# A graph kernel's count matrix: stored by lane in quarters, and block degrees from wide products with a masked sum

## What is computed

```python
def gcn_conv(x, src, dst, W, b):
    n = x.shape[0]
    h = x @ W
    ones = jnp.ones(src.shape[0], dtype=x.dtype)
    deg = jax.ops.segment_sum(ones, dst, num_segments=n)
    dinv = jnp.where(deg > 0, jax.lax.rsqrt(deg), 0.0)
    norm = dinv[src] * dinv[dst]
    msgs = h[src] * norm[:, None]
    out = jax.ops.segment_sum(msgs, dst, num_segments=n)
    return out + b
...
h = gcn_conv(x, src, dst, W1, b1)
h = gcn_conv(h, src, dst, W2, b2)
return jax.nn.relu(h)
```

## Time and profile before

| | us |
|---|---|
| median of 3 runs | 6543.93 |
| lowest, highest | 6538.44, 6555.55 |
| the profiled execution | 6502.53 |
| its span on the page | 6500.8 |

### The profile page before, as it was taken

The page is one execution under the profiler, slowest core; times in us unless marked ns, Lnnn a source line. Parts: engine busy times, 40 slices in busy tenths (PEclk is TensorE's granted clock), DMA queues, the critical chain, the costliest instruction groups (busy, mean ns, idle before and its releaser), DMA issues. The chain is left out here.

```text
span 6500.8 us, 161934 instructions
## 1 busy us (share of the span) xinstructions
PE 4790.6 (74%) x32887; PEld 3107.1 (48%) x32888; DVE 4860.5 (75%) x21938; ACT 3979.7 (61%) x10577; POOL 4009.3 (62%) x5381
## 2 busy tenths in 40 slices
PE   1466666666666666664999999999938888886699
PEld 0233344334343433432555555555525556554699
DVE  6577777777677777773999999999976677777333
ACT  3355555555455545543999999999967777776100
POOL 1277777777677777764666666666627777776000
PEclk8588888878788778876999999999969999998799
DMA  8755556556455555555333333333317777775698
GB/s 224 239 186 182 186 193 197 184 191 194 160 188 174 175 170 167 176 162 160 72 72 72 72 73 74 73 73 73 73 37 216 217 217 223 213 219 174 258 360 344
DMA packets 1161941, 1090.82 MB, mean 168 GB/s; under 512 B 750004, under 2 KB 1023523, under 8 KB 1142980
## 3 DMA queue, kind: packets, MB, share of 16 engines
q1 hardware_dynamic: 1033656, 684.89, 38.9%
q0 software_dynamic: 88560, 320.26, 13.2%
q10 hardware_dynamic: 39580, 84.01, 3.4%
HBM read 658.14 MB, written 430.64 MB: 167 GB/s over the span
## 5 line engine op out<-in xcount | busy, mean ns | idle before, releaser
L914 POOL DMA_INDIRECT rows<-rowS,idx x1616 | 1949.0, 1206 | 787.9 <-issue 441.0
L1185 PE MATMUL psa<-one_c,one_s 128*128 128x392 bf16 x2352 | 605.1, 372 | 762.8 <-DVE one_s L996 461.4
L2425 PE MATMUL psm<-msg,onem 128*128 128x260 f32 x3648 | 918.0, 395 | 205.9 <-issue 169.7
L1694 DVE CUSTOM_DVE_ANT_0 junk<-bufh,attb 128x64 bf16<-128x64 f32 x5472 | 1043.5, 238 | 14.1 <-ACT bufh L1742 6.4
L2346 POOL TENSOR_TENSOR msg<-oj,heads 128x512 f32<-128x512 f32 x760 | 799.3, 1074 | 208.7 <-DMA oj<-rows 176.3
L988 DVE TENSOR_TENSOR one_c<-ioc,pairS 128x1176 bf16<-128x1176 f16 x784 | 598.4, 763 | 433.4 <-remote 227.7
L2425 PEld LDWEIGHTS psm<-msg,onem 128*128 128x128 f32 x3648 | 649.6, 190 | 474.0 <-issue 397.7
L1078 ACT ACTIVATE lgS<-preS 128x1024 f32<-128x1024 f32 x404 | 413.4, 1023 | 617.4 <-PE preS L1174 268.3
L1071 ACT ACTIVATE cnts<-psa 128x392 bf16<-128x392 f32 x784 | 366.8, 490 | 661.2 <-remote 344.3
L1782 PE MATMUL pre<-P3h,oneT 128*128 x5472 | 757.0, 275 | 0.0
L1659 POOL TENSOR_SCALAR one<-io128b,side 128x128 bf16<-128x128 bf16 x912 | 695.7, 763 | 67.2 <-DMA side<-rows 41.0
(11 more groups left out here) (306 smaller groups left out, 9392.0 us busy)
## 6 DMA issues: line engine op xcount, KB each, us to landing
oj<-rows SPq DMA_DIRECT2D x912, 256.0 KB
adj<-adj SPq DMA_DIRECT2D x70, 1568.0 KB, 9.7
adj<-cnts ACTq DMA_DIRECT2D x49, 1568.0 KB
side<-rows SPq DMA_DIRECT2D x912, 69.0 KB, 2.3
bufh<-rows SPq DMA_DIRECT2D x912, 64.0 KB, 2.3
eaS<-in_edge_attr_dram SPq DMA_DIRECT2D x201, 256.0 KB
low<-dlow SPq DMA_DIRECT2D x202, 252.0 KB
adj_early<-adj SPq DMA_DIRECT2D x28, 1568.0 KB, 8.7
```

The lines of the kernel that those rows point to most:

```text
L914: eng.indirect_dma_start(out=m["rows"][h], out_offset=bass.IndirectOffsetOnAxis(ap=idx[s][:, k:k + 1], axis=0), in_=rows[s][:, k, :], in_o ...
L1185: mm = eng.matmul(psa[r][:, 0:z.GC], one_s[r][:, k, :], one_c[r][:, k, :], start=(k == 0), stop=(k == GT - 1))
L1694: ins = eng.tensor_tensor_reduce(junk[q][:, k * H + h, 0, :], buf[j][:, k, 1, h * D:(h + 1) * D], attb[:, 1, h, :], 1.0, 0.0, ALU.mult, AL ...
L2425: mm = eng.matmul(psm[j][:, 0:C + H], one[q][:, k, :], msg[q][:, k, :], start=(k == 0), stop=(k == UT - 1))
```

## The change

`cnts` is laid out by lane, [128 lanes, 49 source blocks]. A copy of ACT now fills 8 whole lanes, 392 numbers in a row in each partition, and reads its PSUM tile with the two dimensions swapped. So a quarter of the lanes (LANES = 32) is complete after each step, and ACT issues a store of that quarter (392 KB) at the end of every step, after waiting for its own copies. The tile in DRAM and the tiles that conv_stage loads have the same layout; a product there takes its weights as `adj[j][:, :, s]`, one number in every 49.

The degrees no longer use each part as weights. Twelve matmuls of four source blocks (512 columns) and one of a single block (128), with the square of ones as weights and `cnts` as moving operand, sum into the PSUM tile `turned`, in which every partition then has the column sums. They stand at the end of step 0, after its last count matmul. In step 1, after `rank`, DVE multiplies `turned` with the identity repeated DEG = 4 times and sums the 512 products of each partition. PE's next use of `turned` that could run into this, the turn for step 2, waits for DVE's product.

```diff
@@ spread_stage, vector
-                if closes(b, s):
-                    eng.wait_ge(deg_ready, b)
-                    eng.tensor_copy(m["deg"][:, span(b - 1, 1)], psr[:, (K + 1) * HB:(K + 1) * HB + 1])
...
+            def degrees(b):
+
+                eng.wait_ge(deg_ready, b)
+                eng.wait_ge(deg_kept, b)
+                eng.tensor_tensor(degm[:, :, :], turned[:, :, :],
+                                  m["ident"][:, None, :].to_broadcast([P, DEG, P]), ALU.mult).then_inc(deg_read, 1)
+                eng.wait_ge(deg_read, b)
+                eng.tensor_reduce(m["deg"][:, span(b - 1, 1)], degm[:, :, :].rearrange("p c l -> p (c l)"), AX.X,
+                                  ALU.add).then_inc(deg_kept, 1)
...
                 rank(b, s, h, between)
+                if closes(b, s):
+                    degrees(b)
@@ spread_stage, scalar
-                        wait(eng, stored[u], b // 2 * 16)
+                        wait(eng, stored[u], b // 2 * 16 * NR_BUF)
...
-                eng.activation(cnts[u][:, :, GQ * s + q, :], psa[r][:, 0:z.GC].rearrange("p (t d) -> p t d", d=GD),
+                eng.activation(cnts[u][:, span((GQ * s + q) * GD, GD), :],
+                               psa[r][:, 0:z.GC].rearrange("p (t d) -> p d t", d=GD),
                                ACT.Copy).then_inc(copied[q], 1)
...
-                    if s == NR_BUF - 1:
-                        for q in range(GQ):
-                            eng.wait_ge(copied[q], step(b, s) + 1)
-                        to = m["adj"][b] if isinstance(b, int) else m["adj"][bass.ds(b, 1)].rearrange("o p c -> (o p) c")
-                        eng.dma_start(to, cnts[u][:, :, :, :].rearrange("p s g d -> p (s g d)")).then_inc(stored[u], 16)
+                    for q in range(GQ):
+                        eng.wait_ge(copied[q], step(b, s) + 1)
+                    to = m["adj"][b] if isinstance(b, int) else m["adj"][bass.ds(b, 1)].rearrange("o p c -> (o p) c")
+                    eng.dma_start(to[:, s * LANES * NB:(s + 1) * LANES * NB],
+                                  cnts[u][:, s * LANES:(s + 1) * LANES, :].rearrange("p l c -> p (l c)"))\
+                       .then_inc(stored[u], 16)
@@ spread_stage, tensor
+                if s == 2 and (not isinstance(b, int) or 0 < b <= NB):
+                    eng.wait_ge(deg_read, b)
...
-                if closes(b, s):
-                    for q in range(GQ):
-                        eng.wait_ge(copied[q], t - 1)
-                    for c in range(NB):
-                        mm = eng.matmul(psr[:, (K + 1) * HB:(K + 1) * HB + 1],
-                                        cnts[1 - u][:, c, :, :].rearrange("p g d -> p (g d)"), m["onesb"][:, 0:1],
-                                        start=(c == 0), stop=(c == NB - 1), skip_group_check=True)
-                    mm.then_inc(deg_ready, 1)
...
+            def degrees(b, u):
+
+                for q in range(GQ):
+                    eng.wait_ge(copied[q], NR_BUF * b)
+                eng.wait_ge(evacuated, NR_BUF * b + 2)
+                for c in range(0, NB, DEG):
+                    n = min(DEG, NB - c)
+                    mm = eng.matmul(turned[:, 0:n, :], m["onesb"][:, :],
+                                    cnts[u][:, :, c:c + n].rearrange("p l c -> p c l"),
+                                    start=(c == 0), stop=(c + n == NB), skip_group_check=True)
+                mm.then_inc(deg_ready, 1)
...
                 if u is not None:
                     adj(b, s, 3)
+                if s == 0 and (not isinstance(b, int) or 0 < b <= NB):
+                    degrees(b, 1 - (after_u if u is None else u))
@@ conv_stage, tensor
             def product(n, j, s):
-                return eng.matmul(place(j), adj[j][:, s, :], parts[n][:, s, :, :].rearrange("p r d -> p (r d)"),
+                return eng.matmul(place(j), adj[j][:, :, s], parts[n][:, s, :, :].rearrange("p r d -> p (r d)"),
                                   start=(s == 0), stop=(s == NB - 1))
```

More of the change, by code:

```diff
@@ L45 @@
 GQ = GB // NR_BUF
+LANES = GQ * GD
 CODE = 1024
@@ L48 @@
 WIDE = 4
+DEG = 4
 EXACT = 256
@@ L258, in gnn_kernel @@
             message_stage(nc, z, m, sb, ps, sem)
-            m["early"] = [sb(top, f"adj_early{j}", [P, NB, P], bf16, side="right") for j in range(EARLY)]
+            m["early"] = [sb(top, f"adj_early{j}", [P, P, NB], bf16, side="right") for j in range(EARLY)]
             node_stage(nc, z, m, sb, ps, sem, W1)
@@ L757, in spread_stage @@
         one_c = [sb(ctx, f"one_c{r}", [P, GT, z.GC], bf16) for r in range(2)]
-        cnts = [sb(ctx, f"cnts{u}", [P, NB, GB, GD], bf16) for u in range(2)]
+        cnts = [sb(ctx, f"cnts{u}", [P, P, NB], bf16) for u in range(2)]
         turned = ps(ctx, "turnedS", [P, K // 2, P], fp32)
@@ L774, in spread_stage @@
             "pre_ready", "exp_done", "out_ready"))
-        deg_ready = sem(ctx, "deg_ready")
+        degm = sb(ctx, "degm", [P, DEG, P], fp32)
+        deg_ready, deg_read, deg_kept = (sem(ctx, n) for n in ("deg_ready", "deg_read", "deg_kept"))
         stored = [sem(ctx, f"adj_stored{u}") for u in range(2)]
@@ L1051, in _ @@
                 eng.memset(oh[j][:, K, :], 0.0).then_inc(cleared, 1)
+            eng.memset(degm[:, :, :], 0.0).then_inc(deg_kept, 1)
             hots(0, 0)
@@ L1127, in _ @@
             for u in range(2):
-                eng.wait_ge(stored[u], (NB + 1 - u) // 2 * 16)
+                eng.wait_ge(stored[u], (NB + 1 - u) // 2 * 16 * NR_BUF)
         @block.tensor
@@ L1138, in turn, with count @@
                 mm.then_inc(turned_ready, 1)
-            def count(b, s, u):
+            def count(b, s):
                 j = s % 2
@@ L1201, in body @@
                 if exists(*nxt):
-                    count(*nxt, (after_u if u is None else u if s < NR_BUF - 1 else 1 - u))
+                    count(*nxt)
                 if u is not None:
                     adj(b, s, 3)
+                if s == 0 and (not isinstance(b, int) or 0 < b <= NB):
+                    degrees(b, 1 - (after_u if u is None else u))
             def one(b, u):
@@ L1215, in _ @@
             turn(0, 0)
-            count(0, 0, 0)
+            count(0, 0)
             rounds(eng, NB // 2, two)
@@ L2512, in _ @@
             for j in range(EARLY):
-                eng.dma_start(m["early"][j][:, :, :].rearrange("p s d -> p (s d)"), m["adj"][j]).then_inc(adj_in, 16)
+                eng.dma_start(m["early"][j][:, :, :].rearrange("p d s -> p (d s)"), m["adj"][j]).then_inc(adj_in, 16)
             eng.wait_ge(adj_in, 16 * EARLY)
@@ L2664, in conv_stage @@
         parts = [m["parts0"], sb(ctx, "parts1", [P, NB, PARTS, D], bf16)]
-        adj = m["early"] + [sb(ctx, f"adj{j}", [P, NB, P], bf16) for j in range(EARLY, BC)]
+        adj = m["early"] + [sb(ctx, f"adj{j}", [P, P, NB], bf16) for j in range(EARLY, BC)]
         bias = [sb(ctx, f"cb{n}", [P, D], fp32) for n in range(2)]
@@ L2704, in load @@
                     a = m["adj"][b] if isinstance(b, int) else m["adj"][bass.ds(b, 1)].rearrange("o p c -> (o p) c")
-                    eng.dma_start(adj[j][:, :, :].rearrange("p s d -> p (s d)"), a).then_inc(adj_in[j], 16)
+                    eng.dma_start(adj[j][:, :, :].rearrange("p d s -> p (d s)"), a).then_inc(adj_in[j], 16)
             for j in range(EARLY, BC):
-                eng.dma_start(adj[j][:, :, :].rearrange("p s d -> p (s d)"), m["adj"][j]).then_inc(adj_in[j], 16)
+                eng.dma_start(adj[j][:, :, :].rearrange("p d s -> p (d s)"), m["adj"][j]).then_inc(adj_in[j], 16)
             eng.wait_ge(w_zero, 1)
```

2 lines of the change are left out of this document (1 added, 1 removed).

## The result

The changed kernel takes **6784.64 us** (median; 6781.08 to 6797.31) where the kernel before takes 6541.18 beside it: a ratio of 1.0378, 95% interval 1.0347 to 1.0409. It is slower by 243 us. The prediction said 6372, 6290 to 6640. Where the runs of one kernel fall into two groups more than 1.5% apart, a ratio compares the faster group alone.

What follows compares the result with a forecast made beforehand. DVE with its stalls (39.8 + 13.9 us a block) was the bound, POOL (48.7) next. Blocks going from 53.75 to 50.2 us over 49 blocks, convolutions 0, gave 6544 - 172 = 6372 us; range 6290 to 6640.

Steps and rivals of the forecast that it cites:

- Part (3): Degrees on PE: 13 wide matmuls replace 49 one-column ones, taking 2.7 to 5.5 us a block, 10.3 at the slow end.
- Rival D: Degree matmuls crawl and the stall before the ranks stays: 57.5 us a block, +184 us, 6728 us; chance 0.08.
- Part (5): DVE's 7.41 us stall before L967 comes from PE's one-column burst, perhaps with the store, and goes.
- the gain of 172 us: Whole forecast saving, all in the first stage: blocks fall from 53.75 to 50.2 us, over 49 blocks.
- Without the stalls POOL sets the block: First stage: once DVE's stalls go, POOL's 32 scatters set a block of 49.7 us, 50.2 with waits left over.
- Part (1): Store of 1568 KB split into four of 392 KB: pair-load waits go, ACT's extra at least 1 us a block.
- Part (2): Copy into cnts (L1071) with strided PSUM read: taken as 0.49 us, bounds 0.4 to 0.98.
- Part (4): DVE's degree product and sum over 512 numbers: at most 726 and 716 ns, +1.3 us a block.
- Part (6): Convolutions: strided weight loads stay hidden under the 82.5 ns product, costing 0; bound 130 ns, +228 us.
- rivals B and C: Convolutions paced by strided loads: 107 ns a product, 6490 us (chance 0.13); or above 118 ns, bound 6600 us (0.10).

Runs made afterwards that it cites:

- e9: Changed kernel with its 13 degree matmuls replaced by 22, two for each of eleven ways to read 512 counts; degrees in effect left out: 6955.3 us.
- e18: The changed kernel as it is, run once more for a trace without "remote" waits: 6390.22 us, ratio 1.0307 to the kernel before.
- e4: The changed kernel without anything of the degrees, which are set to a constant once: 6416.38 us, ratio 0.9887 to the kernel before.
- e3: The kernel before without anything of the degrees, which are set to a constant once: 6421.18 us, ratio 0.9906 to the kernel before.
- e19: The kernel before as it is, run once more for its own trace, without "remote" waits: ratio 0.999 to the kernel before at 6200.25 us.
- e15: The same kernel as e6, timed again in five rounds while the kernel before took 6178.21 us: 6159.51 us, ratio 0.9973.
- e6: The changed kernel, computing everything, but each degree matmul walks its four columns innermost: 6437.25 us, ratio 0.992 to the kernel before.
- e5: The changed kernel, computing everything, but each degree matmul reads ten whole lanes against a band of ones: 6435.55 us, ratio 0.991 to the kernel before.

## Why the prediction was wrong, by its own steps

**Part (3), the degrees, is the step that failed.** It took 2.7 to 5.5 us a block, kept 10.3 "for the range", and put the loss at nothing since POOL would cover them; they take 13.58, and POOL doesn't cover that. The choice rested on "a matmul is not known to read four columns at once", and the factor of 3.8 was carried over from weight loads, whose strided 64 ns per 128 columns are 0.5 ns a column. The moving operand pays 1.09 us / 512 = 2.1 ns. No row of the trace before could have told this: every bf16 matmul of 128 or more columns that follows its like there runs at 0.42 to 0.44 ns a column at full clock. The Trainium skill (SBUF — State Buffer, the paragraph on cachelines) says that each new 16-byte line costs a penalty and that two hits to a line are enough for full bandwidth. e9 agrees on the line: no loss at 4 bytes of step, the full loss from 16 on. It differs on the two hits: at 8 bytes of step, two numbers to a line, a matmul takes 430 ns at full clock against 215, and only at half clock (452 against 379 to 427) is the loss small. The prediction had cited the rule and then let POOL cover the result; its "some 5.4 us or more" is worked out from no row, and the 13.58 measured is 2.5 times as much.

**Rival D had half of the mechanism.** It said that the degrees crawl, which they do, and that the stall in front of the ranks stays, which it did not: "remote" there fell from 167.1 to 30.9 us. Without the stall, it said, POOL would hide them with 8.7 us to spare. With no "remote" waits, e18 shows about 8 us hidden. But 12.2 had to be. With the "remote" waits present less was hidden: 59.4 us a block stand against the 52.2 of e4, so 7.2 of 13.6 are lost. D's sum, 6728, is nearest to the result and had been left out of the range. Its nearness is in part luck: it kept a stall that went and gave DVE 5.5 us of waiting for the degrees, where 310.3 / 38 = 8.2 were measured.

**Part (5), the burst as cause of the stall, is wrong.** e3 has no burst and nearly as much waiting for "remote", at another place (350 us in all against 383). e19 has the burst and no stall. A place in the program was taken for a cause; the prediction said so itself ("an inference from place"). With it falls the gain of 172 us: taking all the degrees away gave 63.

**"Without the stalls POOL sets the block" is right, at another time.** Its 50.2 us used a mean of 1.247 us a scatter, from the rule that a scatter takes 1.31 us while DVE works and 0.96 while it stands. The rule isn't borne out: in e19 DVE is busy 0.85 of the stretch, which by it gives 1.256, and a scatter takes 1.177. In e19 and e18 a scatter takes 1.177 and 1.227 us and a block 47.1 and 51.5. (POOL's idle beyond "issue", too, was 270 / 44 = 6.1 us a block, not "near 5".) With the "remote" waits present, no edit here brought the block under 51.9.

**Part (1)** is right as far as it goes: pair waits went from 96.1 to 33.2 us, and from 144.6 to 52.6 in e19 and e18. Without the "remote" waits they bought nothing that can be seen, since POOL sets the block: e15, with the quarter stores, has the block of e19, 47.1. **Part (2)**: 490 ns, as taken. **Part (4)**: 692 and 685 ns, under the bounds of 726 and 716. **Part (6)** and so rivals B and C: the load took 141 ns (145 was foreseen), the product 82.5, and the bound of 130 ns was not reached. Loads that are 43 ns longer changed nothing: each still starts 83 ns behind the one before it and takes 141, so two of them overlap in the records.

## What to carry to other kernels

The times of a matmul's moving operand go by separate pieces of 16 bytes: one that gives a single number costs 1.7 to 2.5 ns, four to six columns of 0.42 ns at full clock, and as much at half. If a layout must be turned, walk at least four 2-byte neighbours innermost (e6) or let the weights pick the rows (e5). When a transposed layout is weighed, price the reader on the engine that all others queue behind, and price it before counting on another engine to hide it. Don't carry a factor from weight loads over to moving operands. A stall that the profile gives to "remote" and that stands behind a conspicuous instruction is no evidence against that instruction: take the instruction out once and see whether the total of such waits falls, and run the same kernel again at another time.

The version that beats both kernels in both conditions is e6, by less than 1%: 0.992 (0.9877 to 0.9964) with the "remote" waits, 0.9973 (0.9959 to 0.9988) without. Where the last 0.3% comes from isn't shown, as the block is the same 47.1 us.

## What the runs showed of the hardware

The map of e9 was new in its numbers: that a wide stride costs the same at either clock, and that steps of 96 bytes (1.26 us) are dearer than 64 (0.86) or 98 (1.1), for which no run has a reason.

The other surprise is what "remote" stood for. The trace records when an increment of a semaphore arrives. In the kernel before, of 1026 such increments by PE that could be matched between 408 and 2700 us (the first one behind a matmul's recorded end and ahead of the next end for the same semaphore), 334 arrive more than 0.5 us after that end, some by over 10 us; the median is 0.015. In e4, without degrees, it is 470 of 937. For DVE and ACT it is none, and from 3200 us on none on any engine. In e19 it is none of 1275 up to 2500 us. They come in bunches: in one block of e5 the increments of two groups of matmuls whose records end 0.96 us apart (three count matmuls, then the nine rank matmuls) arrive 0.10 us apart, 3.7 and 2.9 us late, and with them DVE, ACT and SP all start again. The row on DVE reads only

```profile
2048.78 0.77 DVE L990 TENSOR_TENSOR one_c<-ioc,pairS 128x1176 bf16<-128x1176 f16 x1 [4.65 <-remote]
```

Late increments stand in this one stage in each of the 14 traces that were taken while the kernel before took 6484 us or more, and in none of the six taken while it took 6178 to 6200, one and the same chip being among both.

Two more things go with them. First, PE itself stands still where it has nothing to wait for. The burst of 49 one-column matmuls takes 1.37 us in every block of e19; in the first trace of the kernel before it takes longer in nearly half of the blocks, up to 20 us, for instance (start, us, then the idle time):

```profile
1516.85 0.94 PE L1149 MATMUL psr<-onesb,cnts 128*128 128x1 bf16 x32
1518.03 0.19 PE L1149 MATMUL psr<-onesb,cnts 128*128 128x1 bf16 x2 [0.25 <-issue]
1518.77 0.52 PE L1149 MATMUL psr<-onesb,cnts 128*128 128x1 bf16 x15 [0.54 <-issue]
```

So the burst does lose time in this condition, though it doesn't make the condition. Second, records are missing there: of the increments by PE, DVE and ACT in the kernel before, 17, 37 and 31% have none, against at most 4% in e19, so the counts above are of what was recorded. As the trace models the ends of matmuls, a late increment can also be a matmul that ended late. Whether it is PE or the semaphores that are held up, what holds them, whether the taking of the trace has a part in it, and what makes the condition, stays open; nothing here was able to bring it about or to end it.
